# Attention scores of a graph layer: a sixth PSUM bank, TensorE four pairs ahead, shorter unread products

## The reference, cut to what matters

```python
h = jnp.einsum('ni,hio->nho', x, W)
hs = h[src]
hd = h[dst]
diff = hd - hs
a1, a2, a3, a4, a5 = jnp.split(a, 5, axis=1)
lin = (a1 . hs) + (a2 . hd) + (a3 . diff) + (a4 . |diff|) + (a5 . hs*hd)   # each summed over d, per head
alpha = jnp.where(lin > 0, lin, ALPHA_SLOPE * lin)
```

## Time and profile before

| | us |
|---|---|
| median of 3 runs | 3046.38 |
| lowest and highest | 3035.77, 3063.17 |
| the profiled execution | 3030.92 |
| its span, first to last instruction | 3029.2 |
| mean granted share of TensorE's clock | 0.823 |

### The profile page before, as it was taken

How to read it: one execution, slowest core, us unless ns; L and a number is a source line. 1 busy time by engine, 2 the same in 40 slices (tenths; PEclk the granted TensorE clock), 3 DMA queues, 4 the chain that set the end, 5 groups by cost and what they waited for, 6 DMA issues and landing times. The chain is left out here.

```text
span 3029.2 us, 59910 instructions
## 1 busy us (share of the span) xinstructions
PE 2165.7 (71%) x15045; PEld 1786.7 (59%) x15046; DVE 1635.9 (54%) x4124; ACT 1448.1 (48%) x3571; POOL 1399.8 (46%) x1397
## 2 busy tenths in 40 slices
PE   4889854455445699999456777777777588859990
PEld 3756443233323599999346666666666477649990
DVE  8899732233323733333555556555565788773346
ACT  6789633223222434343364444444445588643335
POOL 0000366666666133333245555555555299725550
PEclk9999876666666799999778778777788699979995
DMA  2300145433334311111245556555566288582223
GB/s 101 120 22 23 53 148 174 121 93 92 91 92 83 125 35 38 35 38 31 104 136 168 163 165 174 172 171 169 163 177 161 92 269 267 164 297 69 70 67 137
DMA packets 182513, 368.87 MB, mean 122 GB/s; under 512 B 30426, under 2 KB 67716, under 8 KB 182126
## 3 DMA queue, kind: packets, MB, share of 16 engines
q1 hardware_dynamic: 118489, 208.65, 20.5%
q0 software_dynamic: 53760, 148.67, 18.8%
q10 hardware_dynamic: 10133, 9.97, 1.0%
HBM read 275.35 MB, written 91.83 MB: 121 GB/s over the span
## 5 line engine op out<-in xcount | busy, mean ns | idle before, releaser
L830 POOL DMA_INDIRECT scores_rows<-h_gnn,all_slot_dst x440 | 431.4, 981 | 375.8 <-ACT scores_ends L2136 237.3
L882 POOL DMA_INDIRECT weightsL_w<-y_gnn,all_slot_dst x440 | 421.9, 959 | 362.6 <-POOLq L81 157.7
L926 PE MATMUL sum_ps<-weightsL_w 128*128 128x256 f32 x880 | 306.1, 507 | 307.0 <-DVE sums_acc L939 190.7
L926 PEld LDWEIGHTS sum_ps<-weightsL_w 128*128 128x128 f32 x880 | 212.2, 255 | 400.7 <-issue 364.6
L939 DVE TENSOR_TENSOR sums_acc<-sums_acc,sum_ps 128x256 f32 x440 | 185.3, 421 | 428.2 <-remote 209.2
L2077 PE MATMUL scores_diff_ps<-scores_minus,scores_node 128*128 128x128 bf16 x2640 | 351.6, 245 | 84.2 <-issue 83.1
L2077 PEld LDWEIGHTS scores_diff_ps<-scores_minus,scores_node 128*128 128x128 bf16 x2640 | 288.3, 123 | 141.4 <-issue 116.7
L1584 ACT ACTIVATE sums_acc<-expertsL_hid_ps,expertsL_b 128x128 f32<-128x128 f32 x704 | 197.6, 372 | 299.0 <-PE expertsL_hid_ps L1533 241.1
L1533 PE MATMUL expertsL_hid_ps<-sums_acc,expertsL_w 128*128 128x128 f32 x2816 | 335.8, 276 | 3.6 <-DVE sums_acc L1604 2.8
L895 ACT ACTIVATE weightsL_w<-all_count_f,all_slot_src 128x128 f32<-128x128 f32 x440 | 133.5, 387 | 416.8 <-remote 285.0
L2075 PE MATMUL scores_diff_ps<-all_ident,scores_rows 128*128 128x128 f32 x880 | 306.3, 348 | 32.5 <-issue 32.3
(11 more groups left out here) (436 smaller groups left out, 4310.8 us busy)
## 6 DMA issues: line engine op xcount, KB each, us to landing
saved_gnn<-scores_rows SPq DMA_DIRECT2D x220, 264.0 KB
sum_rows<-saved_gnn SPq DMA_DIRECT2D x220, 264.0 KB, 3.2
weightsL_w<-in_L_ffn_W SPq DMA_DIRECT2D x16, 1024.0 KB
weightsL_w<-in_L_ffn_w SPq DMA_DIRECT2D x32, 512.0 KB, 9.0
scores_lanes<-slot_lanes SPq DMA_DIRECT2D x44, 320.0 KB
sort_low_b<-low_lanes SPq DMA_DIRECT2D x32, 416.0 KB, 3.6
weightsL_w<-ys_L SPq DMA_DIRECT2D x6, 1280.0 KB, 11.6
weightsL_w<-y_gnn,all_slot_dst POOLq DMA_INDIRECT x440
```

The costliest lines, as they stand in the source:

```text
L830: pool.indirect_dma_start(out=self.rows[s] if isinstance(self.rows, list) else self.rows[:, s, :], out_offset=None, in_=table[:, :], in_of ...
L882: pool.indirect_dma_start(out=g.rows[k % SLOTS], out_offset=None, in_=table[:, :], in_offset=bass.IndirectOffsetOnAxis(ap=e["slot_dst"][:, ...
L926: last = nc.tensor.matmul(ps[s // 2 % banks][:, s % 2 * D:(s % 2 + 1) * D], pick[h][:, s % HALF, :], g.rows[s], start=True, stop=True)
```

## The change

`diff_ps` and `size` get six places in place of five (`DEEP`), used in turn over all pairs (`deep(i, p)`); `joint` keeps five. The sixth bank is that of the unread products. These now have 256 columns, write columns 240 to 495 of the bank of `sum_ps` that the reduction uses, and are issued ahead of the wait for `joined`. `lead` becomes 4, so that TensorE's order is `differ(n + 4)`, `reduce(n)`. VectorE's order stays.

```diff
--- before.py
+++ after.py
@@ -1991,6 +1991,7 @@
 
     turns = Q // SLOTS
     HP = HALF // 2
+    DEEP = 6
     PARTS = 3
     WP = PARTS * HEADS
     with Names(nc, "scores") as m:
@@ -1998,7 +1999,7 @@
         lanes = m.sb("lanes", [P, 2, HALF * P], FP16)
         minus = m.sb("minus", [P, 2, HALF * P], BF16)
         node = m.sb("node", [P, PAIRS, 2, PARTS, HROW], BF16)
-        size = m.sb("size", [P, HP, 2, KD, P])
+        size = m.sb("size", [P, DEEP, 2, KD, P])
         joint = m.sb("joint", [P, HP, 2, P])
         ends = m.sb("ends", [P, 2, HALF, HEADS])
         total = m.sb("total", [P, HALF, HEADS])
@@ -2006,7 +2007,7 @@
         W = QP * HEADS
         NB = W // 512
         IN = 512 // P
-        diff_ps = [m.ps(f"diff_ps{s}") for s in range(HP)]
+        diff_ps = [m.ps(f"diff_ps{s}") for s in range(DEEP)]
         sum_ps = [m.ps(f"sum_ps{s}") for s in range(2)]
         lanes_in = [m.sem(f"lanes_in{s}") for s in range(2)]
         saved = [[m.sem(f"saved{s}{part}") for part in range(2)] for s in range(2)]
@@ -2019,15 +2020,17 @@
         def by_block(n):
             return size[:, n % HP, :, :, :].rearrange("p j f e -> p (j f e)")
 
-        def halves(p):
-
-            return diff_ps[p % HP][:, :].rearrange("p (j f e) -> p j f e", j=2, f=KD)
+        def deep(i, p):
+            return (PAIRS * i + p) % DEEP
+
+        def halves(i, p):
+
+            return diff_ps[deep(i, p)][:, :].rearrange("p (j f e) -> p j f e", j=2, f=KD)
 
         def chunk(row, f):
 
             return row[:, f:D:KD]
 
-        idle_ps = m.ps("idle_ps")
         with nc.Block() as block:
             @block.sync
             def _(sp):
@@ -2071,7 +2074,7 @@
                     for j in range(2):
                         s = 2 * p + j
                         for f in range(KD):
-                            out = diff_ps[p % HP][:, (KD * j + f) * P:(KD * j + f + 1) * P]
+                            out = diff_ps[deep(i, p)][:, (KD * j + f) * P:(KD * j + f + 1) * P]
                             nc.tensor.matmul(out, chunk(g.rows[:, s, :], f), c["ident"][:, :], start=True, stop=False, is_transpose=True)
                             for part in range(PARTS):
                                 last = nc.tensor.matmul(out, chunk(node[:, p, j, part, :], f), minus[:, s // HALF, s % HALF * P:(s % HALF + 1) * P],
@@ -2081,7 +2084,10 @@
                 def reduce(i, p, last_turn=False):
                     if p % HP == 0:
                         pe.wait_ge(kept, 2 * i + p // HP + 1)
-                    pe.wait_ge(joined, HP + PAIRS * i + p + 1)
+                    if not last_turn:
+                        nc.tensor.matmul(sum_ps[p // HP][:, HALF * WP:HALF * WP + 2 * P].rearrange("p (r e) -> p r e", e=P), c["ones_b"][:, :],
+                                         c["before_b"][:, :].unsqueeze(1).to_broadcast([P, 2, P]), start=True, stop=True)
+                    pe.wait_ge(joined, DEEP + PAIRS * i + p + 1)
                     pe.sem_inc(tick, 1)
                     for j in range(2):
                         s, half = 2 * p + j, p // HP
@@ -2089,8 +2095,6 @@
                         nc.tensor.matmul(out, minus[:, half, s % HALF * P:(s % HALF + 1) * P], node[:, p, j, :, D:HROW], start=True, stop=False)
                         last = nc.tensor.matmul(out, joint[:, p % HP, j, :], c["by_head"][:, :], start=False, stop=True)
                     last.then_inc(reduced, 1)
-                    if not last_turn:
-                        idle_products(nc, c, idle_ps, 1)
 
                 for n in range(NB):
                     pe.wait_ge(spread_out, n + 1)
@@ -2100,7 +2104,7 @@
                         last = nc.tensor.transpose(diff_ps[n % HP][:, i * P:(i + 1) * P], by_block(n)[:, i * P:(i + 1) * P], c["ident"][:, :])
                     last.then_inc(nodes_turned, 1)
                 pe.wait_ge(named, NB)
-                lead = 3
+                lead = 4
                 pe.sem_inc(reduced, PAIRS)
                 for p in range(lead):
                     differ(0, p)
@@ -2140,7 +2144,7 @@
                         act.wait_ge(diffed, PAIRS * i + p + 1)
                         act.wait_ge(joined, PAIRS * i + p + 1)
                         act.sem_inc(tick, 1)
-                        nc.scalar.activation(size[:, p % HP, :, :, :].rearrange("p j f e -> p (j f e)"), diff_ps[p % HP][:, :], ACT.Abs).then_inc(absed, 1)
+                        nc.scalar.activation(size[:, deep(i, p), :, :, :].rearrange("p j f e -> p (j f e)"), diff_ps[deep(i, p)][:, :], ACT.Abs).then_inc(absed, 1)
                         f = p // HP
                         if p % HP == 3:
                             release(i, f, 0)
@@ -2149,7 +2153,7 @@
                         act.wait_ge(absed, HP + PAIRS * i + p + 1)
                         act.sem_inc(tick, 1)
                         for f in range(KD):
-                            last = nc.scalar.activation(halves(p)[:, :, f, :], size[:, p % HP, :, f, :], ACT.Identity,
+                            last = nc.scalar.activation(halves(i, p)[:, :, f, :], size[:, deep(i, p), :, f, :], ACT.Identity,
                                                         bias=coef[:, 0, f:f + 1], scale=coef[:, 1, f:f + 1])
                         last.then_inc(sized, 1)
 
@@ -2183,13 +2187,13 @@
 
                 def multiply(i, p):
                     ve.wait_ge(sized, PAIRS * i + p + 1)
-                    nc.vector.tensor_tensor(size[:, p % HP, :, 0, :], size[:, p % HP, :, 0, :], halves(p)[:, :, 0, :], ALU.mult)
-                    nc.vector.tensor_tensor(halves(p)[:, :, 1, :], size[:, p % HP, :, 1, :], halves(p)[:, :, 1, :], ALU.mult)
+                    nc.vector.tensor_tensor(size[:, deep(i, p), :, 0, :], size[:, deep(i, p), :, 0, :], halves(i, p)[:, :, 0, :], ALU.mult)
+                    nc.vector.tensor_tensor(halves(i, p)[:, :, 1, :], size[:, deep(i, p), :, 1, :], halves(i, p)[:, :, 1, :], ALU.mult)
 
                 def join(i, p):
                     ve.drain()
                     ve.wait_ge(reduced, PAIRS - HP + PAIRS * i + p + 1)
-                    nc.vector.tensor_tensor(joint[:, p % HP, :, :], size[:, p % HP, :, 0, :], halves(p)[:, :, 1, :], ALU.add).then_inc(joined, 1)
+                    nc.vector.tensor_tensor(joint[:, p % HP, :, :], size[:, deep(i, p), :, 0, :], halves(i, p)[:, :, 1, :], ALU.add).then_inc(joined, 1)
 
                 def half(i, f, first=False, last=False):
 
@@ -2217,7 +2221,7 @@
                 ve.sem_inc(g.freed, 4)
                 ve.sem_inc(kept, 2)
                 ve.sem_inc(minus_ready, 2)
-                ve.sem_inc(joined, HP)
+                ve.sem_inc(joined, DEEP)
                 tiles = tiles_of(nc, nc.vector.engine, e, 0, HALF)
                 choose(0, 0)
                 for p in range(HP):
```

## The result

The changed kernel takes 3131.77 us (median of 4 runs, 3128.25 to 3138.92), the kernel before 3046.8 us (4 runs): ratio 1.0288, 95% interval 1.0258 to 1.0319. The change costs 2.9%. The forecast of 3041 us was wrong and its range, which ended at 3106, doesn't hold the result. What happened is rival 3, keep in the freeze, to which I gave 0.11 and 3112 us.

What follows compares the result with a forecast made beforehand. The loop of gathers, products, Abs and freeing copy was taken to bound `scores`. Terms -10 + 0 - 5 + 10 = -5 us took the profiled 3030.9 to 3026; 15.5 us up to the median gave 3041 us, range 2988 to 3106.

Steps and rivals of the forecast that it cites:

- rival 3: VectorE's keep moves to the freeze's end, 6 us late; a quarter staying in 44 halves is +66, 3112 us; chance 0.11.
- the freeze: In `scores`, TensorE's results go unseen from some 3 us into GpSimd's gather series until some 1.5 us after it.
- (d): VectorE's keep waits for sums issued behind one more pair; one Abs later in a third of 17 halves, +10 us.
- (a): Halving the unread columns of 210 TensorE products shortens ScalarE's 49 waits by at most 0.2 us each: -10 us.
- (b): TensorE four pairs ahead: at most its 24.1 us wait for joined sizes can go, but the wait moves; taken as 0.
- R: The moment keep can begin on VectorE (1818.26), from which the issue of pair n+4 was counted.
- (c): Sixth bank and sixth size buffer: ScalarE's 6.3 us wait for the joint buffers reaches one pair further back, -5 us.
- 1a: TensorE's pace sets the stretch of `scores`, so 23 and 24 us both count: 2999 us; chance 0.24.
- 1b: One more pair done when a freeze begins or ends, one Abs less before the copy: 75 us, 2971 us; chance 0.08.
- Rival 2: Halves of six plus four gathers become ten in a row, 3.2 us longer in 17 halves: 3100 us; chance 0.14.
- Rival 4: Fewer unread columns leave one more pair a half at TensorE's lower clock: +53, 3099 us; sign under 0.75; chance 0.05.
- queue of 64: TensorE's instruction queue, not the lead, caps what is issued ahead in a freeze, so a fourth pair adds nothing there.

Runs made afterwards that it cites:

- e4: The kernel before with only the unread products changed (256 columns, in the sums' bank, ahead of the wait), on the fast chip: 2744.39 us, ratio 0.9982.
- e9: The changed kernel with TensorE three pairs ahead again, against the kernel before: 3037.09 us, ratio 0.9993.
- e8: The changed kernel with three buffers of `minus`, five places of `size` and keep two pairs later, against the kernel before: 3041.41 us, ratio 1.0007.
- e6: The kernel before with one move, the last reduction of each half issued behind one more pair's differences: 3116.33 us, ratio 1.029.
- e7: The changed kernel with the last reduction of each half ahead of the fourth pair's differences, against the kernel before: 3018.2 us, ratio 0.9936.
- e10: The changed kernel as it is, run again as the yardstick against the kernel before: 3133.94 us, ratio 1.031.
- e1: The changed kernel with TensorE three pairs ahead again, on the fast chip, against the kernel before: 2745.21 us, ratio 0.9996.
- e12: The kernel before with a memset of 64 columns and a drain on GpSimd after every second gather of the scores: 3374.46 us, ratio 1.1075.

## Why the prediction was wrong

**The step that failed is (d), keep behind one more pair.** I saw that the sums would be issued "just where the freeze sets in", and that was right. I then priced it at +10 us (ends 0 and +29) by two assumptions. The first, that only the split halves are touched, "about 17", and a third of them: it is every half of the stretch shown (41 waits in 830 us; 23 series of ten gathers in a row and 19 split ones in the kernel before, so the split halves were about as many as I had counted; in the half above, the series of gathers began 1.6 us before VectorE came to keep). The second, that VectorE's 242.0 us of idle time hide it. They did hide much: keep waits 355.9 us and the stretch grows by 86.5. But idle time in the list of waits is a sum over 73 places, and the new wait is about 9 us (355.9 / 41) in one place, ahead of the staging that TensorE waits for. What doesn't fit in there is 86.5 / 44 = 2.0 us a half, and it reaches the copy through TensorE, which starts the staged pair late and at half the clock.

**Rival 3** had the mechanism and nearly the price: 1.5 us in each of 44 halves, +66; measured 2.0, +86.5. Its sign in the profile ("VectorE's L2165 waits long for the sums") is the second line of the new list. The 1.5 us was a quarter of 6, and for the quarter I had no row: that 2.0 us of a wait of 8.7 us stayed, again about a quarter, is luck. The rival deserved the greatest chance. Its own condition, "where the sums of pair n-2 are issued later than 3 us into a series", was met by the times that step (d) itself gave: sums issued 1819.3 to 1819.9, a series begun at 1816.18.

**(a), half the unread columns.** The sizes were right: at the full clock the next product starts 2022.62 - 2022.51 = 0.11 us behind an unread one. The -10 us can't be confirmed: alone, without the freeze, 0.9982 with an interval up to 1.0002 (e4), and with the sixth bank 0.9993 (e9).

**(b), four pairs ahead.** Right at 0 for the lead in itself (e8 1.0007). TensorE's wait for the joined sizes, 24.1 us before, isn't among the waits shown any more, as forecast; it came back as 267.8 us ahead of the differences. I had worked that wait out (staged at R + 2.8), but with an R only 1.3 us later. R came some 9 us later.

**(c), sixth bank.** Worth nothing (e9). The waits of ScalarE that the list puts down to the join rose from 6.3 us, 2 times, to 11.7 us, 5 times, but the one in the half above isn't a wait for it.

**Rivals 1a and 1b** didn't happen: the time rose, and ScalarE's "remote" fell only from 296.1 to 268.3 us.

**Rival 2** had its sign right and its reason wrong. Counted in GpSimd's timeline (a gap over 1.2 us ends a series), the kernel before has 23 halves of ten gathers in a row and 19 split ones, the changed kernel 29 and 13, e6 only unsplit ones. But in e8, where TensorE runs just as far ahead, they are 21 and 21, and e7 has even more split ones, 25 to 17. So the split series don't vanish because TensorE is early; in these traces, one of each kernel, they go where keep waits long. This is only a part of the loss in the changed kernel: both kinds of halves got longer, the unsplit ones from 18.9 to 20.8 us on the mean and the split ones from 16.6 to 18.3. These means also show that my 3.2 us a half, read from one half of each kind, was too much; it is 2.3. How much of e6's loss comes in this form, no run tells apart.

**Rival 4**: the clock of the stretch fell to 0.73, under the 0.75 that I had named as its sign. The short unread products aren't the cause: e8 has them, a clock of 0.76 from 1575 to 2362 us and no loss, and e6 has the old ones of 512 columns, a clock of 0.75 and the whole loss. Low clock does take part where TensorE starts again after its wait, as the window above shows (0.50).

The sentence on the queue of 64 (the Trainium skill, TensorE: Matmul & The Clock Gate, table of specifications) is neither borne out nor refuted by the result. TensorE stood at a wait for staged rows, ahead of any cap of a queue. My count of 32 products and 32 weight loads was no evidence for it either: it runs across a wait of TensorE for the join, so the issue wasn't at full pace up to 1804.

```profile
1802.05 0.17 PE L2089 MATMUL scores_sum_ps<-scores_node,scores_minus 128*128 128x24 bf16 x1 [1.31 <-DVE scores_joint L2192]
```

## What to carry to other kernels

Running an engine further ahead puts its older work behind its newer work. For every result of that older work ask who waits for it, and what stands behind the waiting instruction on its engine; here it was one reduction in five whose reader was in a hurry, and issuing just that one ahead of the extra pair turned +3.1% (e10) into -0.6% (e7).

Idle time in a list of waits is no cover for a single long wait: set the new wait against the slack at its place, in each turn.

## What the runs showed of the hardware

The same kernel took 2745.77 us on one chip and 3027 to 3047 on others. Of the fast chip there are traces of e1 to e4 alone, and e1 to e4 can't be told from it in time. In e1 no engine waits for "remote", and the 88 copies take 560.2 us from first to last in place of the 765.6 of the kernel before where the freeze is. So some 205 of the 300 us lie in `scores`. Such waits stand in a later stage of the kernel before too, where GpSimd gathers as well:

```profile
ACT weightsL_w L895 <- remote: 285.0, 26, 20.4
DVE sums_acc L939 <- remote: 209.2, 42, 9.5
```

I didn't take that stage apart, and what makes the chips differ stays open. In the freeze, the results of TensorE were seen late while GpSimd issued gathers; an empty 2.45 us on GpSimd after every second gather made that vanish, and 0.12 us of memset in the usual gap didn't.

The two gathers ahead of a drain show that a gather's row isn't its transfer: in e12 the second one's row ends at 1903.11 + 0.96 = 1904.07, and TensorE's transpose starts at 1906.00, after a wait that the trace puts down to that DMA:

```profile
1906.00 0.46 PE L2079 MATMUL scores_diff_ps<-all_ident,scores_rows 128*128 128x128 f32 x1 [1.15 <-DMA scores_rows<-h_gnn,all_slot_dst]
```

That is 1.93 us. The Trainium skill (Perfetto Trace Analysis, DMA Instruction — SWDGE (GPSIMD)) says that such a row ends when the descriptors have been written, not when the data has moved, and the trace agrees.
